# A recurrent step whose second half makes r and n as products of their own

## The reference

```
gi = x @ W_ih + b_ih
gh = h @ W_hh + b_hh
r = sigmoid(i_r + h_r)
z = sigmoid(i_z + h_z)
n = tanh(i_n + r * h_n)
h_new = (1.0 - z) * n + z * h
```

## Time and profile before

| | |
|---|---|
| median of 3 runs | 2117.36 us (2115.9 to 2118.0) |
| span of the profiled execution | 2113.7 us |
| TensorE busy | 2071.9 us (98%) |
| VectorE busy | 1354.9 us (64%) |
| ScalarE busy | 1239.1 us (59%) |
| GpSimd busy | 638.0 us (30%) |
| mean granted TensorE clock | 0.997 of 2.4 GHz |

### The profile page before, as it was taken

How to read it: one execution, slowest core, us unless ns; L and a number is a source line. 1 busy time by engine, 2 the same in 40 slices (tenths; PEclk the granted TensorE clock), 3 DMA queues, 4 the chain that set the end, 5 groups by cost and what they waited for, 6 DMA issues and landing times.

```text
span 2113.7 us, 181503 instructions
## 1 busy us (share of the span) xinstructions
PE 2071.9 (98%) x77848; PEld 1578.9 (75%) x77848; DVE 1354.9 (64%) x6162; ACT 1239.1 (59%) x5995; POOL 638.0 (30%) x1015
## 2 busy tenths in 40 slices
PE   8999999999999999999999999999999999999998
PEld 2222222222499999999999999999999999998887
DVE  4344445444367777777777777777777777776676
ACT  3445544443266666666666666666666666666665
POOL 0355547444112222222222222222222222222222
PEclk9999999999999999999999999999999999999999
DMA  6000000011222222221222222222121212210001
GB/s 259 1 1 1 1 1 1 1 60 31 49 54 53 52 55 52 52 55 49 69 59 55 52 53 53 56 58 66 50 58 50 58 48 60 67 30 11 5 8 20
DMA packets 218082, 96.04 MB, mean 45 GB/s; under 512 B 170216, under 2 KB 213480, under 8 KB 217320
## 3 DMA queue, kind: packets, MB, share of 16 engines
q1 hardware_dynamic: 217032, 92.00, 16.8%
q10 hardware_dynamic: 928, 2.65, 0.3%
HBM read 26.30 MB, written 12.58 MB: 18 GB/s over the span
## 4 chain that ended last, share of the span: by engine, by line
PE 70%; DVE 2%; issue 0%; DMA 0%; ACT 0%; SPq 0%; DVEq 0%
PE ps L1241 64%; PE ps L1274 4%; PE ps L1282 2%; DVE arena L1069 1%; DVE arena L1087 0%; DMA arena<-arena 0%; DVE arena L965 0%; DVE arena L1075 0%; DVE arena L1082 0%; DVE arena L968 0%; ACT arena L1210 0%; SPq L994 0%; DVE arena L1158 0%; DVE seq L1163 0%; DVE seq L1100 0%
## 5 line engine op out<-in xcount | busy, mean ns | idle before, releaser
L1241 PE MATMUL ps<-whh,arena 128*4 128x128 f32 (+1 forms) x65568 | 1451.4, 246 | 13.8 <-issue 1.6
L1241 PEld LDWEIGHTS ps<-whh,arena 128*4 128x4 f32 x65568 | 1293.6, 87 | 112.2 <-DVE arena L1087 25.8
L1069 DVE STREAM_TRANSPOSE arena<-ps 128x64 f32<-128x64 f32 x2048 | 446.4, 284 | 256.1 <-PE ps L1241 237.0
L1199 ACT ACTIVATE arena<-arena 128x8 f32<-128x8 f32 x1024 | 216.1, 211 | 543.4 <-DVE arena L1069 480.1
L455 DVE TENSOR_REDUCE top<-ps 128x2 f32<-128x1024 f32 x128 | 150.8, 1220 | 244.0 <-PE ps L722 244.0
L1174 ACT ACTIVATE ps<-arena 128x128 f32<-128x128 f32 x1026 | 288.9, 282 | 0.5 <-PEq L212 0.4
L1087 DVE TENSOR_TENSOR_SCAN arena<-arena 128x24 f32<-128x24 f32 x1024 | 192.1, 188 | 145.1 <-ACT arena L1210 145.1
L1075 DVE STREAM_TRANSPOSE arena<-ps 128x64 f32<-128x64 f32 x1024 | 257.5, 251 | 9.0 <-PE ps L1241 3.3
L361 ACT ACTIVATE arena<-ps 128x1024 f32<-128x1024 f32 x128 | 124.1, 1021 | 212.7 <-PE ps L798 212.6
L610 PE MATMUL ps<-arena 128*32 128x512 f32 x2048 | 242.7, 595 | 2.7 <-ACT arena L383 2.7
L965 POOL TENSOR_TENSOR arena<-tap,arena 128x128 f32<-128x128 f32 x252 | 102.0, 415 | 430.0 <-DVE seq L1100 430.0
(11 more groups left out here) (99 smaller groups left out, 1268.0 us busy)
## 6 DMA issues: line engine op xcount, KB each, us to landing
arena<-arena SPq DMA_DIRECT2D x216, 114.0 KB, 2.2
arena<-arena SPq DMA_DIRECT2D x112, 128.0 KB
arena<-seq SPq DMA_DIRECT2D x224, 55.0 KB
arena<-gi_d SPq DMA_DIRECT2D x248, 32.0 KB
gi_d<-arena SPq DMA_DIRECT2D x96, 57.0 KB
out<-seq SPq DMA_DIRECT2D x14, 256.0 KB
seq<-in_x SPq DMA_DIRECT2D x3, 1024.0 KB, 15.6
whh<-in_w_hh SPq DMA_DIRECT2D x1, 3072.0 KB, 21.1
```

The costliest lines, as they stand in the source:

```text
L1069: e.transpose(trn[:, h, q].rearrange("p (i c s) -> p c i s", c=2, s=2)[:, :, :, 0], bank[RN[h]][:, 64 * q:64 * q + 64].rearrange("p (c i) ...
L1199: e.activation(r_d0[:, h].rearrange("p (i s) -> p i s", s=2)[:, :, 1], trn[:, h, 0, 0:2 * NH].rearrange("p (i s) -> p i s", s=2)[:, :, 0], ...
L1241: last = e.matmul(bank[dst[h]][32 * G:32 * G + B, 0:n], hv, wv[:, k, gates, G, 64 * h:64 * h + 64], start=False, stop=k2 == 1 and k == C - ...
```

## The change

Four things change inside the step; the number of outputs and the arithmetic stay.

- On TensorE the half-1 product of r and n (64 + 64 columns) is split into one of r and one of n, 64 columns each. r of half 1 goes to bank 6 or 7 by turns (`R1`), n of half 1 to bank 1 (`N1`). `begin` makes r,n of half 0 and r of half 1 alone. The first part of z of half 0 moves ahead of the wait for the second half of the state. n of half 1 is made whole in `end`.
- On VectorE r of half 1 is turned before scan_n of half 0, n of half 1 after it; scan_n of half 1 goes ahead of turning z of half 1, and the filler operation goes in front of scan_h of half 1. The two waits of `scan_n` stand in the other order.
- On ScalarE the tanh of half 1 goes ahead of the sigmoid of z, whose end now releases scan_h of half 1; r and n of half 1 are seeded apart, and z of half 0 is seeded earlier.
- `begin` has one wait left, and semaphores are kept by product.

```
-        RN, RZ, FA, FN = (0, 1), (2, 3), 4, 5
+        RN0, N1, Z, R1, FA, FN = 0, 1, (2, 3), (6, 7), 4, 5
...
                     def scan_n(h):
-                        e.wait_ge(st["s_tr"], n_at[h])
                         e.wait_ge(st["s_sig"], half[h])
+                        e.wait_ge(st["s_tn"], half[h])
...
                     def scan_h(h):
-                        e.wait_ge(st["s_tanh"], half[h])
+                        e.wait_ge(*((st["s_tanh"], half[0]), (st["s_zs"], next_))[h])
...
-                    turn_rn(0)
+                    turn_r(0)
+                    turn_n(0)
                     turn_z(0)
+                    turn_r(1)
                     scan_n(0)
-                    turn_rn(1)
+                    turn_n(1)
                     scan_h(0)
+                    scan_n(1)
                     turn_z(1)
-                    scan_n(1)
+                    gate_op()
                     scan_h(1)
...
                         if s % HALF == 0:
                             e.wait_ge(s_ring[s // HALF], (it + (1 if s else 2)) * (16 * NG))
+                        seed_r1(1 - u, s)
                         reset(0)
-                        e.wait_ge(st["s_tr"], turned[1])
-                        seed_rn(0, s)
+                        e.wait_ge(st["s_tn"], half[0])
+                        seed_rn0(s)
                         update(0)
                         new(0)
                         reset(1)
-                        e.wait_ge(st["s_tr"], turned[4])
-                        seed_rn(1, s)
+                        seed_z(0, s)
+                        e.wait_ge(st["s_tn"], half[1])
+                        seed_n1(s)
+                        new(1)
                         update(1)
-                        new(1)
-                        seed_z(0, s)
                         seed_z(1, s)
                         bring(following)
...
                 def begin(t, u):
-                    half = (count(2 * t + 1), count(2 * t + 2))
-                    e.wait_ge(st["s_h"], half[0])
-                    e.wait_ge(st["s_seed_rn"], half[0])
-                    products(u, RN, rn, 0, 0)
-                    e.wait_ge(st["s_seed_rn"], half[1])
-                    products(u, RN, rn, 1, 0)
+                    e.wait_ge(st["s_h"], count(2 * t + 1))
+                    products(u, RN0, rn, 0, 0, False)
+                    products(u, R1[u], r, 1, 0, False)
 
                 def end(t, u):
                     half = (count(2 * t + 1), count(2 * t + 2))
+                    e.wait_ge(st["s_seed_z"], half[0])
+                    products(u, Z[0], z, 0, 0, False)
                     e.wait_ge(st["s_h"], half[1])
-                    products(u, RN, rn, 0, 1).then_inc(st["s_rn"], 1)
-                    e.wait_ge(st["s_seed_z"], half[0])
-                    products(u, RZ, z, 0, 0)
-                    products(u, RZ, z, 0, 1).then_inc(st["s_z"], 1)
-                    products(u, RN, rn, 1, 1).then_inc(st["s_rn"], 1)
+                    products(u, RN0, rn, 0, 1, True).then_inc(st["s_rn0"], 1)
+                    products(u, Z[0], z, 0, 1, True).then_inc(st["s_z0"], 1)
+                    products(u, R1[u], r, 1, 1, True).then_inc(st["s_r1"], 1)
+                    products(u, N1, n, 1, 0, False)
+                    products(u, N1, n, 1, 1, True).then_inc(st["s_n1"], 1)
                     e.wait_ge(st["s_seed_z"], half[1])
-                    products(u, RZ, z, 1, 0)
-                    products(u, RZ, z, 1, 1).then_inc(st["s_z"], 1)
+                    products(u, Z[1], z, 1, 1, False)
+                    products(u, Z[1], z, 1, 0, True).then_inc(st["s_z1"], 1)
```

More of the change, by code:

```diff
@@ L167, in build @@
         hb = tile([P, 2, 2, HS + 1])
-        trn = tile([P, 2, 2, P])
+        trr = tile([P, 2, 64])
+        trn = tile([P, 2, P])
         trz = tile([P, 2, 64])
@@ L1056, in _, with step @@
             def _(e):
-                def step(t, u):
+                def step(t, u, gate_op):
                     def count(v):
@@ L1061, in step @@
                     h4 = count(2 * t + 4)
-                    n_at = (count(6 * t + 2), count(6 * t + 5))
                     now = count(t + PAD)
-                    def turn_rn(h):
-                        e.wait_ge(st["s_rn"], half[h])
-                        for q in range(2):
-                            e.transpose(trn[:, h, q].rearrange("p (i c s) -> p c i s", c=2, s=2)[:, :, :, 0],
-                                        bank[RN[h]][:, 64 * q:64 * q + 64].rearrange("p (c i) -> p c i", c=2)
-                                        ).then_inc(st["s_tr"], 1)
+                    next_ = count(t + 1)
@@ L1131, in _, with gate_ops @@
                 seed_n(0)
-                for q in range(BODIES):
-                    for v in range(4):
-                        step(4 * q + v, v % 2)
-                        if v == 0 and q and q % 2 == 0:
-                            seed_n(q // 2)
-                        if v == 2:
-                            take_rz(q)
-                        if v == 3 and q % 2 == 1:
-                            take_n(q // 2)
-                for t in range(4 * BODIES, T):
-                    step(t, t % 2)
+                def gate_ops(t):
+                    q, v = divmod(t, 4)
+                    if q >= BODIES:
+                        return
+                    if v == 0 and q and q % 2 == 0:
+                        seed_n(q // 2)
+                    if v == 2:
+                        take_rz(q)
+                    if v == 3 and q % 2 == 1:
+                        take_n(q // 2)
+                for t in range(T):
+                    step(t, t % 2, lambda: gate_ops(t))
                 t, done = T - NB, s_end
@@ L1182, in _ @@
                 e.wait_ge(s_first, 16 * NG)
-                for h in range(2):
-                    seed_rn(h, 0)
+                seed_rn0(0)
+                seed_r1(0, 0)
+                seed_n1(0)
                 for h in range(2):
@@ L1193, in _ @@
                         half = (e.snap(2 * t + 1), e.snap(2 * t + 2))
-                        turned = [e.snap(6 * t + i) for i in range(1, 7)]
                         following = e.snap(t + 1)
                         def reset(h):
-                            e.wait_ge(st["s_tr"], turned[3 * h])
+                            e.wait_ge(st["s_tr"], half[h])
                             e.activation(r_d0[:, h].rearrange("p (i s) -> p i s", s=2)[:, :, 1],
-                                         trn[:, h, 0, 0:2 * NH].rearrange("p (i s) -> p i s", s=2)[:, :, 0],
+                                         trr[:, h, 0:NH],
                                          ACT.Sigmoid).then_inc(st["s_sig"], 1)
                         def update(h):
-                            e.wait_ge(st["s_tr"], turned[3 * h + 2])
-                            e.activation(z_d0[:, h].rearrange("p (i s) -> p i s", s=3)[:, :, 2], trz[:, h, 0:NH],
-                                         ACT.Sigmoid)
+                            e.wait_ge(st["s_tz"], half[h])
+                            op = e.activation(z_d0[:, h].rearrange("p (i s) -> p i s", s=3)[:, :, 2], trz[:, h, 0:NH],
+                                              ACT.Sigmoid)
+                            if h:
+                                op.then_inc(st["s_zs"], 1)
                         def new(h):
@@ L1232, in _, with products @@
                 wv = whh[:].rearrange("p c (q G n) -> p c q G n", q=3, G=NG)
-                rn, z = slice(0, 3, 2), slice(1, 2)
-                def products(u, dst, gates, h, k2):
-                    n = len(range(3)[gates]) * 64
+                r, z, n, rn = slice(0, 1), slice(1, 2), slice(2, 3), slice(0, 3, 2)
+                def products(u, dst, gates, h, k2, stop):
+                    width = len(range(3)[gates]) * 64
                     for k in (2 * k2, 2 * k2 + 1):
@@ L1240, in products @@
                         for G in range(NG):
-                            last = e.matmul(bank[dst[h]][32 * G:32 * G + B, 0:n], hv, wv[:, k, gates, G, 64 * h:64 * h + 64],
-                                            start=False, stop=k2 == 1 and k == C - 1, skip_group_check=True)
+                            last = e.matmul(bank[dst][32 * G:32 * G + B, 0:width], hv, wv[:, k, gates, G, 64 * h:64 * h + 64],
+                                            start=False, stop=stop and k % 2 == 1, skip_group_check=True)
                     return last
@@ L1307, in _ @@
                 e.wait_ge(st["s_clear"], N_CLEAR)
+                e.wait_ge(st["s_seed_rn0"], 1)
+                e.wait_ge(st["s_seed_r1"], 1)
+                e.wait_ge(st["s_seed_n1"], 1)
                 begin(0, 0)
```

38 lines of the change are left out of this document (25 added, 13 removed).

## The result

The changed kernel takes 2120.34 us, median of 12 runs (2118.28 to 2125.47), against 2118.02 us (12 runs, 2115.66 to 2119.09) for the kernel before beside it: ratio 1.0019 [1.0011, 1.0027]. In a second set of runs it was 2117.57 against 2116.51, 1.0008 [0.9999, 1.0017]. So it is 1 to 2 us slower, at the edge of what can be told from no change. The forecast was +14 us. The profiled execution has a span of 2116.5 us, before 2113.7.

The account below looks back on a forecast made before the run. TensorE was taken to wait for scan_h of half 0 through VectorE, half 1's path as tight. Main loop +11, last 64 steps 0, stalls -1, entry +4, seed +0.2: +14, 2131.5 us; own range 2120 to 2138, with rivals 2106 to 2138.

Parts of the forecast that it names:

- What bounds the kernel before: Undisturbed step of 2.97 us: TensorE idles 0.04 us for scan_h of half 0; half 1's path has 0.01 to spare.
- VectorE and ScalarE after: Within a step, scan_h of half 0 comes 0.09 us earlier; scan_h of half 1 at about 1.87, before 2.01.
- TensorE after: TensorE's own work bounds the 448 steps with fillers at 2.955 us; the scan_h path bounds the last 64 at 2.89.
- The branch: At each loop branch behind `begin`, TensorE's array runs dry for 0.17 us (0.12 to 0.19), with 28 instructions ahead.
- The rule weighed there: Skill's 64-deep TensorE queue: all of `begin` would be queued, the branch over at 0.58, and no bubble appear.
- the first rival: The branch stays hidden (deeper queue or earlier compare): -10, 2107 us; chance 0.18.
- Last 64 steps: Second loop, a body of two: 2 x 2.89 + 0.17 = 5.95 us as before; 0, between -4 and +3 us.
- Entry: Entering the loop at the pace of its instruction blocks; body grows from 288 to 352 products, one more block: +4 us (0 to 5).
- Stalls: Short stalls of 4 us in all; those on half 0's path find 0.07 us of slack: -1 us (0 to -2).
- the second: About the same: a bubble near 0.1 at the branch, or an entry that costs nothing; 2117 us; chance 0.12.
- The third: Half 1's path becomes the bound if its scan_h starts later than 2.01 after r,n are turned; 2153 us; chance 0.10.
- the fourth: The loop no longer fits TensorE's instruction memory and blocks are fetched again each round; far over 3000 us; chance 0.02.

Follow-up runs that it names:

- experiment 8: `before_scan_h_first`: the kernel before with scan_h of half 0 put between the turns of r and n of half 1; 2173.91 us, 1.0274.
- experiment 7: Changed kernel with half 0's first z product moved to the end of `begin` and r of half 1 turned behind scan_n of half 0; 2143.4 us, 1.0132.
- r1_first: Changed kernel with the two products of `begin` swapped, r of half 1 first and r,n of half 0 last; 2119.91 us, 1.0019.

## Why the prediction was wrong

- **What bounds the kernel before**: right. Both paths were as tight as read; experiment 8 shows the half-1 path lose as soon as half 0 gains alone.
- **VectorE and ScalarE after**: right in size. scan_n at 0.62 (said 0.62), scan_h of half 0 at 1.07 (1.09 to 1.10), of half 1 at 1.91 (1.87). scan_n of half 1 came at 1.30 instead of 1.21 and the turn of z at 1.41 instead of 1.34; both had room. The turn of n of half 1 was said to be "no longer in the way", but scan_h of half 0 starts 0.18 behind it, 0.02 before the time that I gave by the tanh, and it is the bound once scan_n is earlier (experiment 7).
- **TensorE after**: right. 2.955 forecast for steps with fillers, 2.951 to 2.957 measured, and 2.89 without fillers (2.891). `begin` starts right behind the last filler.
- **The branch**: this step failed. The mechanism was right: the array runs dry while the sequencer is at the branch, new loads come 0.375 after the compare, and the gap goes into the time in full. The size was wrong: 0.17 forecast, 0.058 measured. The failed step is the sentence "The sequencer reaches the branch at the same place, 28 instructions from the end". I took a count from the earlier trace rows, where two products of 128 columns stood ahead of the branch, for a property of the sequencer, and carried it to products of other widths. It is 38 here. The size follows from it: the register instruction starts 0.238 after `begin`, new work comes 0.098 + 0.375 + 0.007 = 0.48 later, at 0.718; the array is through at 0.66. The ten instructions more are 5 loads and 5 matmuls, a group and a quarter of 128 columns, and the sequencer is 0.12 us earlier at the branch: that is the difference between 0.17 and 0.058.
- **The rule weighed there**: the Trainium skill, "TensorE: Matmul & The Clock Gate" (header table), gives a queue 64 deep, and by the estimate worked out from it there would be no gap. The trace doesn't bear that out: 28 or 38 instructions were not started at the branch, and no run shows 64. For the first rival to come true the array would need 0.06 us more of work ahead of the branch than it has.
- **Last 64 steps**: forecast 0, measured -3.1, for the same reason: 2 x 2.89 + 0.065 is 5.845, not 5.95.
- **Entry**: +4 forecast, +4.0 measured (+3.2 in the other profile of the same kernel, so the exact hit is luck). The same reasoning was not applied to the second loop, whose body grows too: +2.3 us (+1.9 in the other profile).
- **Stalls**: forecast 1 us less, 2.2 more in this execution; two profiles of one kernel differ by 1.7 here, so the term is noise at this size.
- **Rivals**: the second, about the same, came true, by its first condition (a smaller bubble). It had 0.12, because the two ends of the bubble, 0.12 and 0.19, both kept the count of 28. A bound must vary the count too: one more group of 128 ahead is worth 0.11 us, the whole difference. The third did not come: scan_h of half 1 starts at 1.91, not past 2.01. Nor did the fourth: the body's instructions came in 6 packets and none was fetched again in its passes.

**What stays open**: why the widths of the last two products set the lead. The rule predicted two kernels that were made to break it, but it is a description. Three places don't fit it: the second loop of `r1_first` (128 behind 64, lead 36 or 37), the second loop of the kernel before (128 behind 128, lead 28 in 13 of 31 passes and 30 to 32 in most others), and `before_scan_h_first`, whose lead is 20. In all three TensorE waits for VectorE or ScalarE in or near `begin`; in the last it waits for a seed in the middle of `begin`, and the branch's register instruction starts only 0.07 us after that wait. But it waits in the changed kernel's second loop too, whose lead of 36 fits. The reason was not found.

## What to carry to other kernels

A loop branch on TensorE's sequencer is hidden only if the array still has as much work as the branch takes, here 0.48 us from its register instruction to the next load; read how far ahead the sequencer is at that very place, and vary the count, not only the prices, for the range. Where products shrink, put a wide one just before the last narrow one, and let the first product behind the branch have no wait of its own: the order alone was worth 27 to 31 us here between two kernels with the same instructions, and the version that has both was 4.7 us faster than the changed kernel. A loop is entered at the pace of its instruction packets, so a longer body costs time once at each entry: count every loop that holds the changed code.

## What the runs showed of the hardware that I had not expected

- The sequencer's lead over the array isn't one number: 28 or 38 loads and matmuls not started at the branch, for the same 96 instructions in two orders (gap 0.253 against 0.057 us).
- One more register instruction with a fulfilled wait between the products of `begin` changed neither lead nor gap (38 and 0.058), while behind the branch a first product with a wait and a register instruction of 59 ns started 0.030 us later than one without the wait and with a move of 29 ns (0.381 against 0.351 us from the compare to the next matmul).
- Instruction packets of a loop not met before come some 4 us apart, while a step needs 2.9: the entry of a loop of only 32 passes cost 2.3 us more with 80 products a step than with 64, though the packets within its slow steps stayed two.
